# Mixture-of-experts tail of a decoder: sorted rows that carry the residual, and output rows scattered into the output itself

## The reference

```python
x = hidden.reshape(-1, 128)                 # layer norm of the 2048 tokens
gates = softmax((x @ wg_red.T) @ wg_unit.T) # 8 experts
indices_s, scores = argmax(gates), max(gates)
for e in range(8):
    h = gelu(x @ w1[e] + b1[e])             # 128 -> 512
    out = out + (indices_s == e) * (h @ w2[e] + b2[e])   # 512 -> 128
result = residual + out * scores
```

## Time and profile before

| what | us |
|---|---|
| median of three executions | 1084.23 |
| the profiled execution's own time | 1089.41 |
| its span, first to last instruction | 1087.7 |
| PE busy in the span | 953.5 (88%) |
| DVE busy | 788.7 (73%) |
| ACT busy | 625.1 (57%) |
| POOL busy | 477.5 (44%) |

### The profile page before, as it was taken

The page is one execution under the profiler, slowest core; times in us unless marked ns, Lnnn a source line. Parts: engine busy times, 40 slices in busy tenths (PEclk is TensorE's granted clock), DMA queues, the critical chain, the costliest instruction groups (busy, mean ns, idle before and its releaser), DMA issues. The chain is left out here.

```text
span 1087.7 us, 21373 instructions
## 1 busy us (share of the span) xinstructions
PE 953.5 (88%) x6170; PEld 494.0 (45%) x6170; DVE 788.7 (73%) x1673; ACT 625.1 (57%) x1543; POOL 477.5 (44%) x734
## 2 busy tenths in 40 slices
PE   3379999999999998799969999999999996796594
PEld 1112233333333334456644555655555563465394
DVE  7788999999999976576646666656666664986653
ACT  3627888888888883222246556566656652432162
POOL 4221554454454471512025444444545443775452
PEclk9858999999999995599989999999999998886697
DMA  3000000000000000053060000000000000000123
GB/s 85 6 19 15 1 2 2 1 0 0 0 0 0 0 1 1 26 213 125 15 193 16 8 9 15 7 7 14 7 7 7 9 1 1 1 1 10 45 78 100
DMA packets 36108, 28.50 MB, mean 26 GB/s; under 512 B 12344, under 2 KB 33248, under 8 KB 36048
## 3 DMA queue, kind: packets, MB, share of 16 engines
q1 hardware_dynamic: 32896, 16.11, 5.7%
q0 software_dynamic: 3152, 11.65, 2.8%
HBM read 15.14 MB, written 12.61 MB: 26 GB/s over the span
## 5 line engine op out<-in xcount | busy, mean ns | idle before, releaser
L655 DVE TENSOR_REDUCE a_nmax<-a_rows 128x2 f32<-128x1024 f32 x256 | 299.1, 1217 | 15.4 <-PE a_rows L497 12.0
L794 ACT ACTIVATE a_probs<-a_turned 128x512 f32<-128x512 f32 x512 | 269.7, 604 | 46.2 <-PE a_turned L519 44.7
L1275 POOL TENSOR_TENSOR a_prob<-a_prob,a_rinv 128x256 f32<-128x256 f32 (+3 forms) x128 | 159.7, 1253 | 173.2 <-DVE a_rinv L1465 172.9
L1458 DVE TENSOR_REDUCE a_nmax<-a_score 128x2 f32<-128x256 f32 (+3 forms) x128 | 105.5, 825 | 125.5 <-PE a_score L1314 121.5
L1412 ACT ACTIVATE a_prob<-a_score,a_nmax 128x128 f32<-128x128 f32 (+3 forms) x256 | 132.5, 523 | 82.6 <-DVE a_nmax L1458 81.4
L519 PE MATMUL a_turned<-a_q,a_qk 32*128 32x512 bf16 x512 | 138.2, 393 | 5.7 <-ACT a_probs L794 3.9
L482 PE MATMUL a_acc<-a_probs,a_vg 128*32 128x512 f32 x1024 | 141.6, 626 | 0.8 <-ACT a_probs L794 0.7
L497 PE MATMUL a_rows<-a_qk 32*128 32x512 bf16 x512 | 111.9, 402 | 13.4 <-DVE a_nmax L655 5.9
L1311 PE MATMUL a_score<-a_k_s,a_q_s 64*128 64x384 f32 (+3 forms) x512 | 103.6, 481 | 2.2 <-ACT a_prob L1412 1.3
L519 PEld LDWEIGHTS a_turned<-a_q,a_qk 32*128 32x128 bf16 x512 | 35.1, 91 | 154.4 <-ACT a_probs L794 128.9
L1471 DVE COPY a_pt<-a_turn 128x128 f32<-128x128 f32 (+3 forms) x224 | 92.1, 447 | 1.4 <-PE a_turn L1325 1.4
(11 more groups left out here) (340 smaller groups left out, 1608.3 us busy)
## 6 DMA issues: line engine op xcount, KB each, us to landing
xs_sorted<-m_blank POOLq DMA_DIRECT2D x9, 975.0 KB, 4.4
m_m_w<-L_ffn_w SPq DMA_DIRECT2D x8, 512.0 KB, 7.8
a_wq<-L_attn_Wq SPq DMA_DIRECT2D x16, 128.0 KB, 2.2
c_xs<-xs_sorted SPq DMA_DIRECT2D x23, 65.0 KB, 1.8
g_X<-x SPq DMA_DIRECT2D x4, 256.0 KB, 3.7
g_m_wgu<-L_ffn_gate_up_proj SPq DMA_DIRECT2D x8, 128.0 KB, 2.1
a_wk<-L_attn_Wk SPq DMA_DIRECT2D x32, 32.0 KB, 2.0
c_yg<-y_tokens SPq DMA_DIRECT2D x4, 256.0 KB, 3.6
```

Source lines behind the costliest of these rows:

```text
L655: dve.tensor_reduce(nmax[i % 2][:, p // 2, (p % 2) * 2:(p % 2) * 2 + 2], rows[n % 2][:, :, :], AX_X, ALU.max, negate=True).then_inc(row_ou ...
L794: act.activation(probs[:, (tb % 2) * 4 + j, :], turned[n % 3][:, :], ACT.Exp, scale=float(HD0) ** -0.5).then_inc(turn_out, 1)
L1275: pool.tensor_tensor(pr, pr, spread(rinv[:, t % RING, :], 2, width), ALU.mult).then_inc(scl, 1)
L1458: dve.tensor_reduce(nmax[:, t % RING, :], score[t % 2][:, :, 0:width], AX_X, ALU.max, negate=True).then_inc(mx, 1)
```

## The change

The sorted row grows from 130 to 258 floats: behind number and score it carries the token's residual, which ACT copies there from `g.X` (`keep_rows`, once for each batch). The blank rows grow likewise. b2 is loaded once, broadcast to all partitions. The matmul of b2 over all tokens, its transpose, the copy on ACT and the four additions on DVE are gone. In the loop DVE forms b2s = b2[expert] * score + residual and then ysb = down * score + b2s, so that a row of `ysb` is a finished output row. POOL scatters it into `out`, with a bound of 2047 on the index: rows with a higher number aren't written. The reading back, the last additions and the stores are gone. Token numbers are converted two tiles at a time.

```diff
-ROW1 = D + 2
+RES1 = D + 2
+ROW1 = RES1 + D
...
-            for n in range(NT):
-                pool.dma_start(b2r[n * E:(n + 1) * E, :], g.dram["L1_ffn_b2"]).then_inc(small_in, 16)
+            pool.dma_start(g.m1_b2[:, :, :].rearrange("p e d -> p (e d)"),
+                           g.dram["L1_ffn_b2"].rearrange("e d -> (e d)").unsqueeze(0).broadcast_to([P, E * D])
+                           ).then_inc(small_in, 16)
...
-            pool.tensor_tensor(g.m1_b2d[:, :, :], spread(b2r[:, :], 1, NT), spread(hmask[:, :], 2, D),
-                               ALU.mult).then_inc(hm, 1)
...
             for i in range(4):
                 sp.wait_ge(y_out[i], 16 * len(range(i, T, 4)))
-            for b in range(B):
-                sp.dma_start(yg[:, SB * b:SB * b + SB, :],
-                             y_d[S * b:S * (b + 1), :].rearrange("(t p) d -> p t d", p=P)).then_inc(back[b], 16)
-            for b in range(B):
-                sp.wait_ge(s_fin, b + 1)
-                sp.dma_start(out[b].rearrange("(t p) d -> p t d", p=P), g.X[:, SB * b:SB * b + SB, :]).then_inc(stored, 16)
-            sp.wait_ge(stored, 16 * B)
...
             def scatter(p, n0, n1):
                 pool.wait_ge(s_pos, p + 1)
+                pool.wait_ge(s_res, n1 // SB)
...
-                pool.wait_ge(s_id, t + 1)
+                pool.wait_ge(s_id, t // 2 + 1)
                 pool.wait_ge(s_ys, t + 1)
-                pool.indirect_dma_start(out=y_d, out_offset=bass.IndirectOffsetOnAxis(ap=token[:, t:t + 1], axis=0),
-                                        in_=ysb[:, t % 4, :], in_offset=None).then_inc(y_out[t % 4], 16)
+                pool.indirect_dma_start(out=out_rows,
+                                        out_offset=bass.IndirectOffsetOnAxis(ap=token[:, t:t + 1], axis=0),
+                                        in_=ysb[:, t % 4, :], in_offset=None, bounds_check=NT * P - 1,
+                                        oob_is_err=False).then_inc(y_out[t % 4], 16)
...
-            pe.transpose(route_t[:, 0:P], rts[:, :, :].rearrange("p n e -> p (n e)"), g.ident[:, :]).then_inc(s_rtt, 1)
...
-                pe.matmul(bias_ps[b % 2], rtt[:, :], g.m1_b2d[:, SB * b:SB * b + SB, :].rearrange("p n d -> p (n d)"),
-                          start=True, stop=True).then_inc(s_bo, 1)
...
+            def keep_rows(b):
+                act.wait_ge(s_x, b + 1)
+                act.activation(xe[:, SB * b:SB * b + SB, RES1:ROW1], g.X[:, SB * b:SB * b + SB, :], ACT.Copy).then_inc(s_res, 1)
...
+                if step in (10, 14, 18):
+                    keep_rows(step // SB - 2)
...
             exp_of(1)
+            keep_rows(3)
...
             def copy_y(t):
-                dve.tensor_copy(token[:, t:t + 1], xs[:, t, D:D + 1]).then_inc(s_id, 1)
+                dve.scalar_tensor_tensor(out=b2s[:, t % 2, :], in0=g.m1_b2[:, bass.ds(expert[t], 1), :].rearrange("p o d -> p (o d)"),
+                                         scalar=xs[:, t, D + 1:D + 2], in1=xs[:, t, RES1:ROW1], op0=ALU.mult,
+                                         op1=ALU.add).then_inc(s_b2, 1)
                 dve.wait_ge(s_dn, t + 1)
+                dve.wait_ge(s_b2, t + 1)
...
-                dve.tensor_scalar(ysb[:, t % 4, :], down[t % 2][:, 0:D], xs[:, t, D + 1:D + 2], None, ALU.mult
-                                  ).then_inc(s_ys, 1)
+                dve.scalar_tensor_tensor(out=ysb[:, t % 4, :], in0=down[t % 2][:, 0:D], scalar=xs[:, t, D + 1:D + 2],
+                                         in1=b2s[:, t % 2, :], op0=ALU.mult, op1=ALU.add).then_inc(s_ys, 1)
...
-            for b in range(B):
-                dve.wait_ge(s_bo, b + 1)
-                x = g.X[:, SB * b:SB * b + SB, :]
-                dve.tensor_tensor(x, x, bias_ps[b % 2].rearrange("p (n d) -> p n d", d=D), ALU.add).then_inc(s_bx, 1)
...
+                if t % 2 == 1 or t == T - 1:
+                    t0 = t // 2 * 2
+                    for q in range(t0, t + 1):
+                        dve.wait_ge(xs_in[q], 16)
+                    dve.tensor_copy(token[:, t0:t + 1], xs[:, t0:t + 1, D]).then_inc(s_id, 1)
...
-                dve.tensor_tensor(x, x, yg[:, SB * b:SB * b + SB, :], ALU.add).then_inc(s_fin, 1)
```

More of the change, by code:

```diff
@@ L1009, in stage_mixture0 @@
         blank = sc.sb("blank", [P, BLANK // P, ROW1])
-        b2r = sc.sb("b2r", [P, D])
-        hmask = sc.sb("hmask", [P, NT])
         s_gu, s_silu, s_h, s_dn, s_x = (sc.sem(n) for n in ("gate_up", "silu", "hidden", "down", "residual"))
@@ L1131, in _ @@
                                blank[:, :, :]).then_inc(blank_d, 16)
-            pool.memset(hmask[:, :], 1.0).then_inc(hm, 1)
+            pool.memset(g.m1_ones16[:, :], 1.0).then_inc(hm, 1)
             pool.wait_ge(hm, 1)
[L1134 to L1140, removed]
             pool.affine_select(out=g.m1_below[:, :], in_=g.m1_ones16[:, :], compare_op=ALU.is_ge, fill=0.0, base=-1,
@@ L1150, in _ @@
                       allow_small_or_imprecise_dtypes=True).then_inc(hm, 1)
-            pool.wait_ge(small_in, 16 * (3 + NT))
-            pool.wait_ge(hm, 9)
-            pool.tensor_tensor(g.m1_b2d[:, :, :], spread(b2r[:, :], 1, NT), spread(hmask[:, :], 2, D),
-                               ALU.mult).then_inc(hm, 1)
-            pool.wait_ge(hm, 10)
+            pool.wait_ge(small_in, 16 * 4)
+            pool.wait_ge(hm, 6)
             pool.wait_ge(blank_d, 16 * (SLOTS1 // BLANK))
@@ L1581, in stage_cross1_mixture1 @@
         ysb = sc.sb("ysb", [P, 4, D])
-        yg = sc.sb("yg", [P, NT, D])
+        b2s = sc.sb("b2s", [P, 2, D])
         warm = sc.sb("warm", [P, 1])
-        xs_d, y_d = g.m1_xs_d, g.m1_y_d
+        xs_d, out_rows = g.m1_xs_d, out.rearrange("b s d -> (b s) d")
         xs_in = [sc.sem(f"xs_in{t}") for t in range(TILES1)]
@@ L1593, in stage_cross1_mixture1 @@
              "up", "hidden", "down", "y_scaled", "final", "stored"))
+        s_b2, s_res = sc.sem("bias_row"), sc.sem("residual_row")
         T = TILES1
@@ L1805, in _ @@
             rank_of(2)
-            pe.wait_ge(s_rts, 1)
-            pe.wait_ge(s_x, B)
-            pe.transpose(route_t[:, 0:P], rts[:, :, :].rearrange("p n e -> p (n e)"), g.ident[:, :]).then_inc(s_rtt, 1)
-            pe.wait_ge(s_rttc, 1)
-            pe.wait_ge(s_pos, 3)
-            for b in range(B):
-                wait(pe, s_bx, b - 1)
-                pe.matmul(bias_ps[b % 2], rtt[:, :], g.m1_b2d[:, SB * b:SB * b + SB, :].rearrange("p n d -> p (n d)"),
-                          start=True, stop=True).then_inc(s_bo, 1)
             def turn_of(t):
@@ L1909, in _ @@
             act.activation(warm[:, :], g.mhalf[:, 0:1], ACT.Gelu)
-            act.wait_ge(s_rtt, 1)
-            act.activation(rtt[:, :], route_t[:, 0:P], ACT.Copy).then_inc(s_rttc, 1)
             act.wait_ge(s_b1, 2)
@@ L2074, in _ @@
             dve.tensor_copy(row_i[:, :], row[:, :]).then_inc(s_map, 1)
-            dve.tensor_tensor(rts[:, :, :], pick16[:, :, :], spread(xe[:, :, D + 1], 2, E), ALU.mult).then_inc(s_rts, 1)
             dve.wait_ge(prep_c, 3)
@@ L2082, in _ @@
             dve.reduce_sum(b1s[:, :, :], b1w[:, :, :, :], AX_X).then_inc(s_b1, 1)
+            expert = {}
             def copy_w1(t):
@@ L2087, in copy_w1 @@
                 wait(dve, s_up, t - 2)
-                e = dve.value_load(eid_i[0:1, t:t + 1], min_val=0, max_val=E - 1)
-                dve.tensor_copy(w1[t % 3][:, :], g.m1_w1[:, bass.ds(e, 1), :].rearrange("p o h -> p (o h)")
+                expert[t] = dve.value_load(eid_i[0:1, t:t + 1], min_val=0, max_val=E - 1)
+                dve.tensor_copy(w1[t % 3][:, :], g.m1_w1[:, bass.ds(expert[t], 1), :].rearrange("p o h -> p (o h)")
                                 ).then_inc(s_w1, 1)
@@ L2171, in decoder @@
             g.m1_b1r = s2.sb("m1_b1r", [E * FC, P])
-            g.m1_b2d = s2.sb("m1_b2d", [P, NT, D])
+            g.m1_b2 = s2.sb("m1_b2", [P, E, D])
             g.m1_ones16 = s2.sb("m1_ones16", [P, P], BF16)
@@ L2179, in decoder @@
             g.m1_xs_d = nc.dram_tensor("xs_sorted", (SLOTS1, ROW1), F32).ap()
-            g.m1_y_d = nc.dram_tensor("y_tokens", (NT * P + SLOTS1, D), F32).ap()
             for stage in (stage_mixture0, stage_attention1):
```

## The result

| | before | changed |
|---|---|---|
| median of 13 executions, us | 1084.23 (1081.31 to 1089.58) | 1079.35 (1075.82 to 1081.84) |
| ratio, 95% interval | | 0.9945 (0.993 to 0.9961) |
| span of the profiled execution | 1087.7 | 1077.8 |
| its own time | 1089.41 | 1079.66 |

The forecast was 1079.5.

What follows compares the result with a forecast made beforehand. PE was taken to set the loop at 1.89 us a tile, with a removable tail of transfers behind it. -7.4 + 2.2 + 0.5 = -4.7 us, 1084.7 profiled; less 5.2 carried over, 1079.5 us, range 1076.0 to 1085.0.

Steps and rivals of the forecast that it cites:

- End, -7.4: Last stage's end: readback, additions and stores go, POOL's drain then ends last, 1078.6 instead of 1086.0; -7.4 us.
- rival B: Stage end and loop start: drain shrinks since fewer rows go out, clock rises quickly; -7.6 us, 1076.6; chance 0.10.
- Clock, +2.2: Loop start on PE: without the b2 matmuls the loop itself must raise the clock from 1.2 GHz; +2.2 us.
- Longer rows, +0.5: Last list scatter and first load of sorted rows: twice the bytes; +0.5 us, bounds 0 and 1.
- DVE, 0: DVE in the loop: with b2s added its period is 1.78 us, under PE's 1.89; 0, upper bound 0 to +2.
- Rival C: Loop: b2[expert]'s address costs an issue gap, DVE becomes the bound at 2.13 a tile; +5.3 us, 1084.8; chance 0.08.
- ACT's copies, 0: Four ACT copies of some 0.6 us where ACT has room; 0, uncovered at most 2.4 us.
- Blank rows, 0: Mixture 0: nine doubled transfers, POOL done at 517 to 538, before the other engines drain at 546; 0.
- D: Loop: b2s and POOL's scatter exclude each other, period 2.4 instead of 1.89; +11 us, 1090.5; chance 0.06.
- E: List scatters cost POOL more with longer rows or a bound; 0.4 us more each cancels the gain, doubled 1093; chance 0.06.

Runs made afterwards that it cites:

- e9: Changed kernel with POOL waiting for all its scatters to land before the stage's barrier: 1080.90 us, ratio to before 0.9964.
- e10: Changed kernel with one added POOL drain once the 16 scatters to the sorted list have landed, ahead of the loop: 1076.3 us, ratio to before 0.992.
- e11: e10 with further POOL drains in the loop, before the scatters of tiles 4, 8, 12, 16 and 20: 1082.48 us, ratio to before 0.9986.
- e2: Changed kernel plus four unused f32 matmuls ahead of the loop to raise PE's clock: 1076.52 us, ratio to before 0.9913.
- e5: Kernel before without its b2 matmuls, the routing's transpose and copy, and the four residual additions: 1086.7 against 1084.31 us, ratio 1.0009.
- e3: Changed kernel with DVE's b1w products and their sum moved behind the w1 copies and the last scatter's landing: 1078.57 us, ratio to before 0.9947.
- e1: The changed kernel run and profiled again without edits: 1078.65 us, ratio to before 0.9946.
- e6: Kernel before with sorted rows of 258 floats, the added ones zero and unused: 1085.18 against 1084.30 us, ratio 1.0009.
- e7: Changed kernel with b2s formed once more in each tile, into a spare tile nobody reads: 1082.57 us, ratio to before 0.9997.

## Why the prediction was right

1. *End, -7.4.* Measured -7.2. The 0.2 that is missing is the bounded scatter: POOL starts it 0.85 us after the end of ysb (1067.88 to 1068.73), before it was 0.75, and it takes 0.98 for 0.96, once each for the last two. The step was right to put the drain, not the landing, at the end; without it the term would have been -9.3. Its reading of the drain as POOL's own work after DMAs holds for this drain, whose length goes with the number of DMAs (e9, e10); a drain close behind few DMAs waits for the landing (e11). The bound "shrinks since fewer rows go out" of rival B falls with it, since skipped rows don't change the number of DMAs.
2. *Clock, +2.2.* Measured +1.85 for all of the loop in the first trace. e2 takes 1.7 of it away, e5 puts 2.0 into the kernel before. The low level ran from the first group at 1024.54 to inside 1028 to 1029, 4.1 us, between the two samples of the earlier trace rows. It changes from execution to execution: 4.1 to 5.0 us in the six traces that start an otherwise unchanged loop low, with 1.9 to 2.6 us lost from the second transpose to the last ysb against the 44.1 before (the changed kernel, e9, e5, e10, e3 and e1, in this order for both; the end of the low level is worked out from the mean clock of the microsecond in which it rises). So the 1.4 to 3.1 was the right kind of bound, and 2.2 lies in the middle of what was seen. The Trainium skill (TensorE: Matmul & The Clock Gate, HAM oscillation) has the loss as the low time times (1 - 1.2/2.4), which makes 2.0 of 4.1 and 2.5 of 5.0, and the traces agree with 1.9 and 2.6. Its Part 1 says that the ramp is under 1% of a typical span and that one shouldn't fit to a count of cold matmuls. That holds here too (2 of 1080 us), but taken as leave to drop the term, as the prediction put it, it would have put the forecast 2.2 us too low.
3. *Longer rows, +0.5.* +0.41, and +0.44 alone in e6. The +0.41 has some luck in it: the list scatter last but one took 1.78 us in the changed kernel's trace and 2.01 before. From the start of the last list scatter to the first transpose it is 5.85 us against 5.24, so +0.6.
4. *DVE, 0.* The period held, and my 1.78 for DVE's own cycle is what e7 gives (1.79). Two errors cancel in it, which is luck: the sum had 0.29 for xst where the next operation starts after 0.20, and 0.29 + 0.05 from b2s to ysb where e7 has 0.43 (1057.62 to 1058.05), since b2s takes 0.35 and ysb waits for it. Rival C was 0.1 us a tile away. Its condition, an issue gap at the expert's address, didn't come: b2s starts 0.20 after xst in a tile without a cast.
5. *ACT's copies, 0.* Three of the four lie ahead of the first list scatter, and from the stage's start to that scatter it is 87.5 us with them (906.8 to 994.3) and 87.7 without (911.6 to 999.3). The fourth took 0.61 us straight behind an exp, and from the first list scatter to the fourteenth it is 19.7 us with it and 19.6 without (994.34 to 1014.00, 999.33 to 1018.96).
6. *Blank rows, 0.* POOL's drain began at 518.8, forecast 517 to 538; e6 has the same stage length as e5.

D fell: the b2s of 1034.62 ran inside a scatter at its usual 0.35. E fell: 0.96 for list scatters of twice the bytes, 0.98 for those to `out`.

The Trainium skill (SBUF — State Buffer, Who interferes with whom) has a DVE operation with two SBUF inputs contend with a GpSimd one that reads SBUF, and the prediction took a scatter for such a one. The same section holds, as an inference, that generating a DMA's descriptors needs the write side of the shared ports, which a DVE operation with two inputs doesn't take. The 0.35 inside a scatter fits that and not the prediction's reading. The slow list scatter beside b1w (1.78 or 2.01 instead of 0.96) may be contention after all, but five traces with b1w in the same place don't have it (1.01 or 1.02), and it isn't settled.

## What to carry to other kernels

When a tail of transfers goes, read the barrier's own line to see which engine was already late under it; a GpSimd that has issued many DMAs drained for 0.08 us each here, and a drain in an idle stretch ahead took 1.2 us off the last drain, while drains inside a busy loop cost more than they saved. Matmuls that lie in a wait aren't always free to remove: look at the granted clock at the start of the dense work that follows. And put the slack of an added operation on one cycle, not on every engine of it.

## What the runs showed of the hardware

- POOL's drain: 1.118, 1.365, 2.343 and 3.247 us for 13, 16, 28 and 39 DMAs issued since the drain before, with all landed, from 0.5 KB to 1935 KB each; with three DMAs, the last in flight, it ended with the landing (e11).
- An indirect DMA cost POOL 0.96 us for 128 rows of 520 or 1032 bytes (1.15 for the first behind other work), 0.98 to `out` with a bound (1.18 in one of 23). What of the 0.02 is the bound and what the other target wasn't tested.
- Between the end of ysb and the start of its scatter POOL lets 0.75 us go by in the kernel before and 0.85 in the changed one.
- The granted clock stayed at 0.50 for 4.1 to 5.0 us of dense matmuls at the loop's start in six traces, and the loop lost 1.9 to 2.6 us by it.
- The same kernel's list scatter last but one took 1.02 us in one execution and 1.78 in another.
